# Edge stage of a graph network: three engines go by pairs of tiles instead of single tiles

## Chip, cores and metric

The kernel runs on one core of one Trainium2 chip. The metric is device time in microseconds (us) of one execution; the chip's runs are given as a median with their lowest and highest value. The output must be that of the reference.

## What is computed

The kernel runs two layers of a graph transformer on 3,125 nodes with 256 features and 100,000 edges. The change touches one stage, the messages of the first layer along the edges. The part of the reference that it computes:

```
src, dst = (edge_index[0], edge_index[1])
ei = jnp.concatenate([x[src], edge_attr], axis=-1)
core = jnp.maximum(ei @ W1 + b1, 0.0) @ W2 + b2
gate = jax.nn.sigmoid(ei @ Wg + bg)
msg = gate * core
agg = jax.ops.segment_sum(msg, dst, num_segments=x.shape[0])
```

Everything else (node tables before it, attention, experts, the second layer) is left as it is.

## The kernel before, in words

`stage_edges` works on 784 tiles of 128 edges (`NET`), four of them in a super (`SUP`), 16 in the body of a loop (`BODY`). The part of the products that depends on the source node lies ready in a table in memory; a tile's rows are gathered from it. Per tile t the work is:

- GpSimd: gather of 128 table rows of 512 numbers (`pool_pass`, L357), into eight slots.
- TensorE `edge_part` (L368, L369): the edge attributes times the weights, two matmuls of 512 columns into one of two PSUM banks.
- VectorE `whole_row` (L469): adds the gathered row, gives Z. With the first tile of a super it also copies the indices of the super after next (`indices`, L461).
- TensorE `turn` (L376): two transposes of the hidden half of Z into one of two PSUM banks.
- ScalarE `high` (L436): relu of it, rounded. ScalarE `gates` (L443): sigmoid of the other half of Z. ScalarE `seed` (L421): writes the bias into the PSUM bank that `core` adds to.
- VectorE `hidden_lo` (L482): what the rounding left over.
- TensorE `core` (L387): six matmuls of 256 columns.
- VectorE `message` (L507): gate times core.
- TensorE `total` (L404): adds the messages to the window of destination nodes, by a one-hot matrix; these two fp32 matmuls show as four records of 64 columns in the trace.

Once per super VectorE builds the one-hot matrices (`near_hots_of`, L499), adds the finished window to the sums (`add_window`, L519), and finishes the attributes of the super after next (`attr_lo`, L475), after ScalarE has rounded them (`rounded`, L451). TensorE's `edge_part` of that super's first tile waits for this L475.

The order is written out by hand: each engine runs `step(k, u)` for every u, and a step does its parts for tiles at fixed distances ahead of u or behind it. Nothing but these steps and the semaphores sets the order. Before the change a step is one tile. TensorE does `turn` of tile u+2, `total` of u-2, `core` of u, `edge_part` of u+4. VectorE does `message` of u-1, `whole_row` of u+3, `hidden_lo` of u+1, then what is due once per super. ScalarE does `high` of u+2, `seed` of u+1, `gates` of u+2. The semaphores let `turn` of tile t begin when `whole_row` of t and `hidden_lo` of t-2 are done, since two tiles share a bank.

Of the kernel before, what the change touches and what calls it, by code (L numbers as in the profile page):

```python
# [262 lines left out]
def stage_edges(c, tag, e):  # L263
# [11 lines left out]
    with ctx:  # L275
# [38 lines left out]
        def loop(step):  # L314


            def whole(eng):
                for u in range(-4, BODY):
                    step(0, u)
                with eng.Fori(1, NB - 1) as k:  # L320
                    for u in range(BODY):
                        step(k, u)
                for u in range(BODY + 3):
                    step(NB - 1, u)
            return whole

        def at(k, u):

            k, u = k + u // BODY, u % BODY
            if isinstance(k, int) and not 0 <= k < NB:  # L330
                return None
            return k, u, k * BODY + u, k * (BODY // SUP) + u // SUP, u // SUP, u % SUP

        def turn_of(k, j):

# [25 lines left out]
        def pe_pass(pe, s, p):  # L361
# [45 lines left out]
                last.then_inc(s["hot_used"], 1)  # L407

            def step(k, u):
                for ahead, part in ((2, turn), (-2, total), (0, core), (4, edge_part)):  # L410
                    a = at(k, u + ahead)
                    if a:
                        part(a)
            loop(step)(pe)

        def act_pass(act, s, p):
            def seed(a):

                k, u, i, sp_, j, q = a
                act.wait_ge(s["msg_ready"], p * NET + i + SLOTS - 1)  # L420
                act.activation(c.ps[4 + u % 2][:, 0:D], b2[:, :], ACT.Copy).then_inc(s["seeded"], 1)  # L421

            def step(k, u):
                a, next_core = at(k, u + 2), at(k, u + 1)
                if a:
                    high(a)
                if next_core:
                    seed(next_core)
                if a:
                    gates(a)  # L430

            def high(a):
                k, u, i, sp_, j, q = a
                act.wait_ge(s["z_turned"], p * NET + i + SLOTS + 1)
                act.wait_ge(s["core_ready"], p * NET + i + 1)
                act.activation(hT_hi[:, u % SLOTS, :, :].rearrange("p b n -> p (b n)"),  # L436
                               c.ps[2 + u % 2][:, 0:KB * 128], ACT.Relu).then_inc(s["h_rounded"], 1)
# [18 lines left out]
        def dve_pass(dve, s, p):  # L456
# [38 lines left out]
            def near_hots_of(a):  # L495

                k, u, i, sp_, j, q = a
                c.fence(dve)
                dve.tensor_tensor(near_hot[:, j % 2, :, :], bc(wide_iota[:, 0:WIN], 1, SUP),  # L499
                                  bc(rel[:, bass.ds(sp_ * SUP, SUP)], 2, WIN), ALU.is_equal).then_inc(s["hot_ready"], 1)  # L500
# [18 lines left out]
                dve.tensor_tensor(cols, cols, acc, ALU.add).then_inc(s["added"], 1)  # L519

            def step(k, u):
                for ahead, part in ((-1, message), (3, whole_row), (1, hidden_lo)):
                    a = at(k, u + ahead)
                    if a:
                        part(a)
                if s is sems[0]:
                    a = at(k, u)
                    if a and a[5] == 0:
                        near_hots_of(a)
                else:  # L530
                    a = at(k, u - 1)
                    if a:
                        far_hot_of(a)

                a = at(k, u)
                if a and a[5] == 2 and not (isinstance(a[0], int) and a[3] + 2 >= NSUP):
                    attr_lo(a[3] + 2, a[4])
                a = at(k, u - 3)
                if a and a[5] == SUP - 1:
                    add_window(a)  # L540
# [2671 lines left out]
```

## Time and profile before

| | us |
|---|---|
| median of 3 runs | 4462.46 |
| lowest and highest | 4461.76 and 4466.28 |
| the profiled execution, its own time | 4470.01 |
| its span, first to last instruction | 4468.2 |
| tiles of this stage, first and last transpose (L376) | 152.3 to 1637.9 |

Busy shares over the whole span: TensorE matmuls 84%, VectorE 66%, ScalarE 47%, GpSimd 48%. The mean granted TensorE clock is 0.905. The stage of the change fills the third of the span from 150 to 1640 us. Rows below name engines as PE (TensorE matmul), PEld (TensorE weight load), DVE (VectorE), ACT (ScalarE), POOL (GpSimd) and SPq (DMA issued by SyncE). In a timeline a row gives start, duration, engine, line, what is written and read, and in brackets idle time of the engine before it with what ended it. The ends of matmuls are modelled, so distances between their starts are what counts.

### The profile page before, as it was taken

What the parts mean: (1) busy time and instruction counts of PE and PEld (TensorE: products, weight loads), DVE (VectorE), ACT (ScalarE), POOL (GpSimd) and SP (SyncE); (2) the same over time, 40 slices, a digit from 0 to 9 for tenths busy, and PEclk for the clock granted to TensorE, in tenths of its full rate; (3) what the DMA queues carried; (4) which work ended last, traced back from release to release, by engine and by line L of the source; (5) the groups of instructions that cost most, each with busy time, mean ns of one, the idle gap of its engine ahead of it and who ended that gap; (6) DMA issues with size and microseconds to landing.
All of it is one profiled execution on the core that took longest, in us unless ns stands there. A gap on an engine that the chain in (4) does not pass through costs nothing. (4 is left out here: it accounts for less than half of the span.)

```text
span 4468.2 us, 86099 instructions
## 1 busy us (share of the span) xinstructions
PE 3749.2 (84%) x22567; PEld 3100.1 (69%) x22567; DVE 2969.3 (66%) x6849; ACT 2099.8 (47%) x4956; POOL 2147.9 (48%) x2102
## 2 busy tenths in 40 slices
PE   7899999999999987998996755556554669999996
PEld 6798988989898986997883433333332558888885
DVE  7699988989998987555332323223231469989998
ACT  3466655656665645774221100000000258888884
POOL 0355555555555521000005666666666257777872
PEclk9899999999999997999998977777876679999998
DMA  4465665666665630003553333333333123332325
GB/s 137 134 176 171 173 174 169 176 171 176 172 177 169 174 97 17 19 14 118 183 184 113 90 90 90 90 90 89 92 88 92 46 68 72 72 74 67 72 51 129
DMA packets 226995, 509.02 MB, mean 114 GB/s; under 512 B 51805, under 2 KB 94299, under 8 KB 220426
## 3 DMA queue, kind: packets, MB, share of 16 engines
q0 software_dynamic: 116736, 313.66, 25.2%
q1 hardware_dynamic: 106389, 187.30, 14.8%
q10 hardware_dynamic: 3679, 5.79, 0.4%
q8 instruction: 87, 1.43, 0.1%
q14 instruction: 104, 0.85, 0.1%
HBM read 434.08 MB, written 72.49 MB: 113 GB/s over the span
## 5 line engine op out<-in xcount | busy, mean ns | idle before, releaser
L775 POOL DMA_INDIRECT big<-table,e_idx x784 | 752.5, 960 | 978.7 <-DVE e_idx L866 589.1
L357 POOL DMA_INDIRECT big<-table,e_idx x784 | 768.4, 980 | 852.2 <-DVE big L469 300.8
L2315 POOL DMA_INDIRECT g_S<-gsrc,g_idx x512 | 608.9, 1189 | 216.5 <-issue 166.4
L436 ACT ACTIVATE e_hT_hi<-psum 128x256 fp32r<-128x256 f32 x784 | 301.1, 384 | 588.1 <-PE psum L376 496.3
L469 DVE TENSOR_TENSOR big<-psum,big 128x512 f32<-128x512 f32 x784 | 539.5, 688 | 45.6 <-PE psum L369 17.1
L896 DVE TENSOR_TENSOR big<-big,psum 128x128 f32 x196 | 56.6, 289 | 763.9 <-PE psum L802 324.5
L825 ACT ACTIVATE e_sums_kept<-psum 64x256 f32<-64x256 f32 x196 | 70.5, 375 | 1040.6 <-DMA gint<-big 429.6
L789 PE MATMUL psum<-big,e_near_hot 128*64 128x256 f32 x1568 | 500.2, 468 | 15.1 <-DMA big<-table,e_idx 14.8
L387 PE MATMUL psum<-e_w_hi,e_hT_hi 128*128 128x256 f32 x1568 | 509.7, 325 | 0.1
L387 PE MATMUL psum<-e_w_hi,e_hT_lo 128*128 128x256 f32 x1568 | 443.5, 283 | 0.0
L802 PE MATMUL psum<-ident,e_sums_kept 64*128 64x64 f32 x392 | 74.1, 278 | 439.4 <-ACT e_sums_kept L825 313.1
L387 PE MATMUL psum<-e_w_lo,e_hT_hi 128*128 128x256 f32 x1568 | 440.6, 281 | 0.0
L404 PE MATMUL psum<-e_near_hot,e_msg 128*128 128x64 f32 x3136 | 438.8, 263 | 0.2 <-DVE e_msg L507 0.2
L802 PEld LDWEIGHTS psum<-ident,e_sums_kept 64*128 64x128 f32 x392 | 45.6, 162 | 537.1 <-issue 537.1
L404 PEld LDWEIGHTS psum<-e_near_hot,e_msg 128*128 128x128 f32 x3136 | 414.3, 192 | 0.3 <-DVE e_msg L507 0.3
L507 DVE TENSOR_TENSOR e_msg<-psum,e_gate 128x256 f32<-128x256 f32 x784 | 331.0, 422 | 88.1 <-PE psum L387 42.8
L2860 PE MATMUL psum<-g_hot,g_spread 128*120 128x262 f32 x2048 | 345.3, 306 | 48.3 <-DVE g_spread L2694 22.7
L789 PEld LDWEIGHTS psum<-big,e_near_hot 128*64 128x64 f32 x1568 | 235.7, 165 | 179.0 <-issue 104.6
L2860 PEld LDWEIGHTS psum<-g_hot,g_spread 128*120 128x120 f32 x2048 | 282.0, 187 | 73.8 <-issue 55.2
L482 DVE SCALAR_TENSOR_TENSOR e_hT_lo<-psum,e_hT_hi 128x256 fp32r<-128x256 f32 x784 | 326.0, 416 | 0.1
L376 PE MATMUL psum<-ident,big 128*128 128x128 f32 x1568 | 305.1, 276 | 22.6 <-DVE e_hT_lo L482 20.7
L443 ACT ACTIVATE e_gate<-big 128x256 f32<-128x256 f32 x784 | 319.3, 407 | 0.0
(421 smaller groups left out, 9434.0 us busy)
## 6 DMA issues: line engine op xcount, KB each, us to landing
big<-in_attr_t SPq DMA_DIRECT2D x392, 128.0 KB
g_rest<-gpart SPq DMA_DIRECT2D x128, 256.0 KB
big<-table,e_idx POOLq DMA_INDIRECT x1568
table<-C SPq DMA_DIRECT2D x26, 896.0 KB
table<-n_rows SPq DMA_DIRECT2D x24, 896.0 KB
experts<-g_region SPq DMA_DIRECT2D x15, 560.0 KB
g_S<-gsrc,g_idx POOLq DMA_INDIRECT x512
table<-big SPq DMA_DIRECT2D x25, 224.0 KB
```

Source lines behind the costliest of these rows:

```text
L357: pool.indirect_dma_start(G[:, j % 2, q, :], None, table, bass.IndirectOffsetOnAxis(idx[:, j, q:q + 1], 0)).then_inc(s[f"G_in{j % 2}{q}"], 16)
L376: last = pe.transpose(c.ps[2 + u % 2][:, b * 128:(b + 1) * 128], Z[:, u % SLOTS, b * 128:(b + 1) * 128], c.ident[:, :])
L387: last = pe.matmul(c.ps[4 + u % 2][:, 0:D], x, y[:, b, :], start=False, stop=b == KB - 1 and x is lo, skip_group_check=True)
L404: last = pe.matmul(acc[:, b, :], msg[:, u % 2, b * 128:(b + 1) * 128], hot, start=q == 0 and (b == 0 or s is sems[1]), stop=q == SUP - 1, ...
L443: act.activation(gate[:, u % SLOTS, :], Z[:, u % SLOTS, D:2 * D], ACT.Sigmoid).then_inc(s["gate_ready"], 1)
L469: dve.tensor_tensor(Z[:, u % SLOTS, :], c.ps[u % 2], G[:, j % 2, q, :], ALU.add).then_inc(s["zs_ready"], 1)
L482: dve.scalar_tensor_tensor(out=hT_lo[:, u % SLOTS, :, :].rearrange("p b n -> p (b n)"), in0=c.ps[2 + u % 2][:, 0:KB * 128], scalar=0.0, in ...
L507: dve.tensor_tensor(msg[:, u % 2, :], c.ps[4 + u % 2][:, 0:D], gate[:, u % SLOTS, :], ALU.mult).then_inc(s["msg_ready"], 1)
L775: pool.indirect_dma_start(G[:, j % n, q, :], None, c.table1, bass.IndirectOffsetOnAxis(idx[:, j, q:q + 1], 0)).then_inc(s[f"G_in{j % n}"], 16)
L789: last = pe.matmul(near_sums(j), onehot[:, q, :], G[:, j % n, q, :], start=q == 0, stop=q == SUP - 1)
L2315: pool.indirect_dma_start(S[:, j, q, :], None, c.gsrc, bass.IndirectOffsetOnAxis(idx[:, j, 0, q:q + 1], 0)).then_inc(w_in[j], 16)
L2860: last = pe.matmul(sums[half], spread[:, j, 2 * u + p, half * CLASSES // 2:(half + 1) * CLASSES // 2, :].rearrange("p k c -> p (k c)"), ho ...
```

## The change

A helper `pair` runs a part for two tiles in a row, and the steps go over every second u. TensorE's step now does `edge_part` of u+4 and u+5, `turn` of u+2 and u+3, `total` of u-2 and u-1, `core` of u and u+1. ScalarE does `seed` of u and u+1, then `high` and `gates` of u+2 and u+3. VectorE does `message` of u-2 and u-1, `whole_row` of u+4 and u+5, `hidden_lo` of u+2 and u+3, then what is due once per super. Buffers, semaphores and their values, GpSimd's and SyncE's programs and the number of compute instructions stay.

```
             def whole(eng):
-                for u in range(-4, BODY):
+                for u in range(-6, BODY, 2):
                     step(0, u)
                 with eng.Fori(1, NB - 1) as k:
-                    for u in range(BODY):
+                    for u in range(0, BODY, 2):
                         step(k, u)
-                for u in range(BODY + 3):
+                for u in range(0, BODY + 4, 2):
                     step(NB - 1, u)
...
+        def pair(k, u, ahead, part):
+
+            for n in range(2):
+                a = at(k, u + ahead + n)
+                if a:
+                    part(a)
...
             def step(k, u):
-                for ahead, part in ((2, turn), (-2, total), (0, core), (4, edge_part)):
-                    a = at(k, u + ahead)
-                    if a:
-                        part(a)
+                for ahead, part in ((4, edge_part), (2, turn), (-2, total), (0, core)):
+                    pair(k, u, ahead, part)
             loop(step)(pe)
...
             def step(k, u):
-                a, next_core = at(k, u + 2), at(k, u + 1)
-                if a:
-                    high(a)
-                if next_core:
-                    seed(next_core)
-                if a:
-                    gates(a)
+                for ahead, part in ((0, seed), (2, high), (2, gates)):
+                    pair(k, u, ahead, part)
...
             def step(k, u):
-                for ahead, part in ((-1, message), (3, whole_row), (1, hidden_lo)):
-                    a = at(k, u + ahead)
-                    if a:
-                        part(a)
-                if s is sems[0]:
-                    a = at(k, u)
-                    if a and a[5] == 0:
-                        near_hots_of(a)
-                else:
-                    a = at(k, u - 1)
-                    if a:
-                        far_hot_of(a)
+                pair(k, u, -2, message)
+                if s is sems[1]:
+                    pair(k, u, -2, far_hot_of)
+                pair(k, u, 4, whole_row)
+                pair(k, u, 2, hidden_lo)
+                a = at(k, u)
+                if s is sems[0] and a and a[5] == 0:
+                    near_hots_of(a)
 
                 a = at(k, u)
                 if a and a[5] == 2 and not (isinstance(a[0], int) and a[3] + 2 >= NSUP):
                     attr_lo(a[3] + 2, a[4])
```

The order on TensorE, at the head of the loop's body (the step of u = 0). Before, the first tile's `turn` (L376) stands first:

```order
L376 MATMUL psum<-ident,big 128x128 x2
L397 ISA
L404 MATMUL psum<-e_near_hot,e_msg 128x64 x2
L383 REGISTER_ALU
L387 MATMUL psum<-e_w_hi,e_hT_hi 128x256
L387 MATMUL psum<-e_w_lo,e_hT_hi 128x256
L387 MATMUL psum<-e_w_hi,e_hT_lo 128x256
```

Three more L387 follow, and then `edge_part` (L368, L369) ends the step.

With the change, from the second `edge_part` of the step on (the first stands just ahead of these rows). In the changed kernel these lines have other numbers: L375 and L376 are `edge_part`, L383 is `turn`, L411 is `total`, L394 is `core`:

```order
L373 REGISTER_ALU
L375 MATMUL psum<-e_wb_hi,e_attr_parts 128x512
L376 MATMUL psum<-e_wb_lo,e_attr_parts 128x512
L381 REGISTER_ALU
L383 MATMUL psum<-ident,big 128x128 x2
L381 REGISTER_ALU
L383 MATMUL psum<-ident,big 128x128 x2
L404 ISA
L411 MATMUL psum<-e_near_hot,e_msg 128x64 x2
L404 REGISTER_ALU
L411 MATMUL psum<-e_near_hot,e_msg 128x64 x2
```

`edge_part` moved from the end of the step to its head, and every part stands there twice before the next part begins.

The order on VectorE in the step that finishes attributes (L475 in both kernels), before and then with the change; L507 is `message`, L469 `whole_row`, L482 `hidden_lo` in both:

```order
L507 TENSOR_TENSOR e_msg<-psum,e_gate 128x256
L465 REGISTER_ALU
L469 TENSOR_TENSOR big<-psum,big 128x512
L482 SCALAR_TENSOR_TENSOR e_hT_lo<-psum,e_hT_hi 128x256
L475 TENSOR_TENSOR e_attr_parts<-big,e_attr_parts 64x512
```

```order
L507 TENSOR_TENSOR e_msg<-psum,e_gate 128x256
L506 REGISTER_ALU
L507 TENSOR_TENSOR e_msg<-psum,e_gate 128x256
L465 REGISTER_ALU
L467 REGISTER_ALU
L469 TENSOR_TENSOR big<-psum,big 128x512
L465 REGISTER_ALU
L467 REGISTER_ALU
L469 TENSOR_TENSOR big<-psum,big 128x512
L482 SCALAR_TENSOR_TENSOR e_hT_lo<-psum,e_hT_hi 128x256 x2
L475 TENSOR_TENSOR e_attr_parts<-big,e_attr_parts 64x512
```

L475 now stands behind two `message`, two `whole_row` and two `hidden_lo` of its step instead of one each. Before, the `edge_part` that waits for it is the last part of the second tile step after it; now it is the first part of the next pair step.

## Rows read from the trace of the kernel before

**Rows 1.** Engines over the span (first part of the page), and the span:

```profile
span 4468.2 us, 86099 instructions
PE 3749.2 (84%) x22567; PEld 3100.1 (69%) x22567; DVE 2969.3 (66%) x6849; ACT 2099.8 (47%) x4956; POOL 2147.9 (48%) x2102
```

**Rows 2.** Windows: stretch, length, busy us of each engine (count), clock, DMA share, GB/s:

```profile
500.00:700.00 200.00, 197.61 (x1476) 179.93 (x1476) 180.88 (x423) 120.56 (x344) 103.03 (x106) 0.99 0.61 173
```

**Rows 3.** Waits, 200 to 1630 us: engine line <- releaser: us, times, longest:

```profile
DVE e_msg L507 <- PE psum L387: 38.5, 57, 3.2
PEld psum L376 <- DVE e_hT_lo L482: 38.4, 120, 2.8
...
PE psum L376 <- DVE e_hT_lo L482: 15.9, 9, 2.4
```

**Rows 4.** Timeline of TensorE, a little over one tile in which nothing stalls:

```profile
801.84 0.40 PE L368 MATMUL psum<-e_wb_hi,e_attr_parts 128*128 128x512 f32 x1
802.07 0.39 PE L369 MATMUL psum<-e_wb_lo,e_attr_parts 128*128 128x512 f32 x1
802.30 0.38 PE L376 MATMUL psum<-ident,big 128*128 128x128 f32 x2
802.52 0.56 PE L404 MATMUL psum<-e_near_hot,e_msg 128*128 128x64 f32 x4
802.89 0.36 PE L387 MATMUL psum<-e_w_hi,e_hT_hi 128*128 128x256 f32 x1
...
803.56 0.28 PE L387 MATMUL psum<-e_w_hi,e_hT_lo 128*128 128x256 f32 x1
803.57 0.19 PEld L368 LDWEIGHTS psum<-e_wb_hi,e_attr_parts 128*128 128x128 f32 x1
803.68 0.39 PE L368 MATMUL psum<-e_wb_hi,e_attr_parts 128*128 128x512 f32 x1
```

**Rows 5.** Timeline of TensorE, first tile of a loop body and of the next:

```profile
584.33 0.39 PE L368 MATMUL psum<-e_wb_hi,e_attr_parts 128*128 128x512 f32 x1
584.56 0.40 PE L369 MATMUL psum<-e_wb_lo,e_attr_parts 128*128 128x512 f32 x1
584.83 0.44 PE L376 MATMUL psum<-ident,big 128*128 128x128 f32 x2
585.11 0.56 PE L404 MATMUL psum<-e_near_hot,e_msg 128*128 128x64 f32 x4
...
586.27 0.39 PE L368 MATMUL psum<-e_wb_hi,e_attr_parts 128*128 128x512 f32 x1
...
614.04 0.39 PE L368 MATMUL psum<-e_wb_hi,e_attr_parts 128*128 128x512 f32 x1
```

**Rows 6.** Timeline of TensorE where another body begins, at half clock:

```profile
765.83 0.63 PE L369 MATMUL psum<-e_wb_lo,e_attr_parts 128*128 128x512 f32 x1
765.89 0.18 PEld L376 LDWEIGHTS psum<-ident,big 128*128 128x128 f32 x1 [0.15 <-DVE e_hT_lo L482]
```

**Rows 7.** Timeline of the three engines at a pause, one of seven:

```profile
560.02 0.40 PE L369 MATMUL psum<-e_wb_lo,e_attr_parts 128*128 128x512 f32 x1
561.34 0.42 DVE L507 TENSOR_TENSOR e_msg<-psum,e_gate 128x256 f32<-128x256 f32 x1 [3.10 <-PE psum L387]
561.36 0.38 ACT L436 ACTIVATE e_hT_hi<-psum 128x256 fp32r<-128x256 f32 x1 [3.30 <-remote]
562.81 0.44 PE L376 MATMUL psum<-ident,big 128*128 128x128 f32 x2 [2.39 <-DVE e_hT_lo L482]
```

**Rows 8.** Windows, one of five stretches at half clock behind a pause:

```profile
563.20:566.50 3.30, 3.30 (x16) 3.00 (x15) 1.89 (x6) 1.51 (x4) 1.89 (x2) 0.50 0.32 79
```

**Rows 9.** Timeline, VectorE, ScalarE and the transpose's weight load:

```profile
800.21 0.40 PE L369 MATMUL psum<-e_wb_lo,e_attr_parts 128*128 128x512 f32 x1
...
800.65 0.69 DVE L469 TENSOR_TENSOR big<-psum,big 128x512 f32<-128x512 f32 x1
...
801.26 0.41 DVE L482 SCALAR_TENSOR_TENSOR e_hT_lo<-psum,e_hT_hi 128x256 fp32r<-128x256 f32 x1
...
801.71 0.69 DVE L475 TENSOR_TENSOR e_attr_parts<-big,e_attr_parts 64x512 fp32r<-64x512 f32 x1
...
802.42 0.29 DVE L519 TENSOR_TENSOR big<-big,psum 128x128 f32 x1
...
802.63 0.42 DVE L507 TENSOR_TENSOR e_msg<-psum,e_gate 128x256 f32<-128x256 f32 x1
802.72 0.38 ACT L436 ACTIVATE e_hT_hi<-psum 128x256 fp32r<-128x256 f32 x1 [0.85 <-PE psum L376]
802.96 0.68 DVE L469 TENSOR_TENSOR big<-psum,big 128x512 f32<-128x512 f32 x1
803.56 0.41 DVE L482 SCALAR_TENSOR_TENSOR e_hT_lo<-psum,e_hT_hi 128x256 fp32r<-128x256 f32 x1
803.94 0.42 DVE L507 TENSOR_TENSOR e_msg<-psum,e_gate 128x256 f32<-128x256 f32 x1
804.03 0.27 PEld L376 LDWEIGHTS psum<-ident,big 128*128 128x128 f32 x2 [0.15 <-DVE e_hT_lo L482]
```

**Rows 10.** Groups of instructions, 200 to 1630 us: count, busy us, mean ns, idle before:

```profile
L499 DVE TENSOR_TENSOR e_near_hot<-big,e_rel 128x256 f32<-128x256 f32 x189 | 78.6, 416 | 0.0
L461 DVE COPY e_idx<-e_src_i 128x4 int32 x187 | 30.1, 161 | 0.0
```

## The prediction, made before the changed kernel ran

> **What bounds the kernel now.** I read the page first: over the span TensorE is busy 84% and VectorE 66% [rows 1], a mean over stages. The stage of the change is read by windows: in 200 us of its middle TensorE is busy 197.6 and VectorE 180.9 [rows 2], at a clock of 0.99. TensorE sets the pace there, with VectorE close behind. The 784 tiles take (1637.9 - 152.3) / 783 = 1.897 us each (first and last transpose, by the table above).
>
> The timeline says what of this is matmuls. A tile in which nothing stalls takes 803.68 - 801.84 = 1.84 us from L368 to L368 [rows 4]: 0.23 and 0.23 for `edge_part`, 0.22 for `turn`, 0.37 for `total` up to the first matmul of `core`, 0.79 for `core`. The loop body of 16 tiles shows one stall that always comes back: its first tile takes 586.27 - 584.33 = 1.94, the 15 after it 27.77, or 1.851 each [rows 5]. So 0.09 to 0.10 us per body is lost at L376, the transposes. The waits name what ends that: `hidden_lo` (L482) of two tiles earlier on VectorE, 120 waits of TensorE's weight load, 38.4 us by this view, which also counts what lies beside running matmuls [rows 3]. The matmul queue itself shows 15.9 us in 9 waits.
>
> Nearly all of those 15.9 us are something else: seven times in the stage, some 200 us apart, VectorE and ScalarE stand still for 3.1 to 3.3 us, and TensorE follows for about 2.4 [rows 7]. Behind five of them the clock falls to 0.50, its level of 1.2 GHz, for 3.3 us [rows 8]: 16 matmuls run where about twice as many would, some 1.7 us lost each.
>
> My account of the stage, over 783 x 1.84 = 1441 us: pauses 7 x 2.4 = 17, half clock 5 x 1.7 = 8.5, body stalls 49 x 0.1 = 4.9. The last 14 of 1485.6 are the filling of the pipe, and 0.01 us per tile of small waits and uneven starts.
>
> **The change, part by part.**
> - *Fewer changes between kinds of matmul.* Worth nothing. A step of two tiles has the same matmuls and weight loads, and none of the starts in [rows 4] has a gap that belongs to a change of kind: L369 to L376 takes 0.23, as L368 to L369 does, though the operand type changes there. The 0.37 of `total` is four records at some 0.11 with the first weight load of `core`, the next 0.79 is six matmuls at 0.12 and the rest of that load. A pair step is then 2 x 1.85 = 3.70 us, and twice the sum of its parts.
> - *`turn` no longer waits for VectorE.* I lay the pair step out from rows, with TensorE's step at 0. L369 of the two `edge_part` start at 0.23 and 0.70, `turn` at 0.93 and 1.15, the last `core` matmuls at 2.86 and 3.58. VectorE: `message` starts 0.38 after such a last matmul (803.56 to 803.94) [rows 4, 9], so at -0.46 and 0.26. `whole_row` can start 0.44 after L369 (800.21 to 800.65) [rows 9]: 0.67, the second 0.61 later at 1.28, `hidden_lo` at 1.89 and, 0.33 later (a short operation's spacing, 802.63 to 802.96), at 2.22. The transposes waiting for that `hidden_lo` come in the next step, at 3.70 + 0.93 = 4.63, and the signal takes 0.47 from its start (803.56 to 804.03) [rows 9]. Slack: 4.63 - 1.89 - 0.47 = 2.27 us, where now there is none in the stalled tiles. The body stalls go: -4.9. Of the small waits I give a third of 0.01 x 783, so -2.6.
> - *`edge_part` at the head of the step.* It waits for `whole_row` of two tiles earlier, 1.28 + 0.75 against 3.70 and more: free. Once per super (196 times) it waits for `attr_lo`, L475, and there the cover becomes thin. L475 starts 0.45 after the second `hidden_lo` (801.26 to 801.71) [rows 9]: 2.67, it takes 0.69 and 0.06 for the signal: 3.42. TensorE wants to load these weights 0.11 ahead of its matmul [rows 4], at 3.59. Slack 0.17 us, with 0 the value that I take. This is the wait that is late next.
> - *ScalarE.* `high` starts 0.31 after the second transpose (802.41, half way through the pair that starts at 802.30, to 802.72) [rows 4, 9]: 1.35, done at 1.73 and with the signal at 1.79, 0.10 ahead of the first `hidden_lo`. `seed` of the second tile follows its `message`, 0.26 + 0.42 + 0.06 = 0.74, done at 1.13; `core` of that tile begins at 2.9. Nothing waits.
> - *VectorE's load.* Per four tiles: 4 x (0.33 + 0.61 + 0.33) = 5.08, attributes and window 0.12 + 0.71 + 0.21 = 1.04 [rows 9], one-hot matrices 0.42 and indices 0.16 at most [rows 10]; 6.70 of 7.40 us. It keeps up, in whatever order.
> - *The loop's branch* was followed by `turn`, behind a matmul of 0.23; now it stands behind one of 0.12. Upper bound: weights are loaded 0.27 after L369's start [rows 5], which with 0.11 for the load would leave 0.26 open, 48 x 0.26 = +12.5. Lower bound 0. In one body `hidden_lo` was early and the load came 0.06 after L369's start [rows 6], so the branch itself is no longer than that; this is the nearest row: 0.06 + 0.11 - 0.12 = 0.05, at most 2.4 us. I take +1.2.
> - *Gathers and attribute transfers* keep their slots and semaphores. No wait of `whole_row` for a gather is among those of [rows 3], and GpSimd is busy 103 of 200 us [rows 2]. Cost 0.
> - *Pauses* stop all other engines; 0, bounded by -7 and +3. *Filling and draining* with pairs: two more `edge_part` ahead of the first `core`, less behind the last; I take +0.1, bounds -2 and +2.
>
> Sum: -4.9 - 2.6 + 1.2 + 0.1 = **-6.2 us**. Against the profiled execution's 4470.0 that is 4463.8; this execution is 7.5 above the median, so the time I predict is 4462.5 - 6.2 = **4456.3 us**.
>
> A rule that speaks against it: VectorE's starts lie closer than its durations (0.61 for 0.69, 0.33 for 0.42) [rows 9]. The Trainium skill ("VectorE: DVE Perf Modes", section "The DRAIN you can't avoid") says that the next operation does not start until the pipe is empty. By that rule four tiles would take VectorE 7.68 us (full durations, worked out under rival 1) in either order, the change would gain nothing, and the time would stay 4462.5. The trace before, with four tiles in 7.40, does not agree; the rule has its chance within rival 1.
>
> **The rivals.**
> 1. *VectorE sets the pace once like operations stand in a row* (two `whole_row`, two `hidden_lo`). No row shows two of a kind in a row. If they need their full durations, four tiles take 4 x (0.42 + 0.69 + 0.42) + 0.69 + 0.29 + 0.42 + 0.16 = 7.68 us instead of 7.40. For it: the durations. Against: the mixed starts. In full that is 196 x 0.28 = +55, but at that length the kernel before would already go slower than it does. The spacing between like operations can be longer than mixed ones by a little, and 0.03 in a pair step, 392 x 0.015 of it on TensorE, eats the gain above. I give "gains and small costs cancel", 4459 to 4466, 0.18. The full price is left out as remote.
> 2. *L475 comes late at the head of the step*: slower. Place: TensorE's first load of every second pair step. It decides from the point where L475 starts later than 2.84 after the step's start, 0.17 later than laid out; a chain of three waits each 0.06 late does it. Price: 0.05 to 0.2 us x 196 = 10 to 39, less the 6 gained: 4466 to 4495, likeliest 0.1 late, 4476. For it: the thinnest cover of all, and VectorE often 0.08 behind its shortest spacing. Against: VectorE catches up 0.3 us in the pair step between. Chance 0.14.
> 3. *The pauses get shorter and the clock stays up.* With 1 to 2 us of slack in every buffer TensorE runs on while the others stand: 7 x 1 us, and without a gap as long five stretches of half clock may go, 8.5. Then 4456 - 7 - 8.5 = 4441. For it: slack grows from 0 to 2.27 at the transposes. Against: the slack at L475 does not grow, and VectorE must still make good 3 us of work. Chance 0.15.
> 4. *The change does not do what it says*: the order of instructions shows that it does. Under 0.01.
>
> **How the numbers follow.** Forecast 0.53, its own range 4451 to 4461; rival 1 0.18, rival 2 0.14, rival 3 0.15. A measurement of this kernel can tell 0.2% from no change, 8.9 us. Faster by more than that is under 4453.5: rival 3 and a third of the forecast's share, 0.15 + 0.18 = 0.33. Slower by more is over 4471.4: most of rival 2 and a remnant of full price of rival 1, 0.15. Within: 0.52. The range reaches half into rivals 2 and 3: 4443 to 4475.
>
> **What would show it.** Right: 16 tiles in 29.5 to 29.6 us in stretches without a pause (29.71 now), no wait of `turn` for `hidden_lo` except at pauses, seven pauses of TensorE of 2 to 2.6 us. Wrong: a group of waits of `edge_part` for L475, some 98 or 196 of them (rival 2); VectorE without idle time and `total` or `core` waiting for it (rival 1); a first `edge_part` of each body 0.2 us late (the branch); the clock at 1.00 throughout (rival 3). The forecast would fall if two like operations on VectorE start more than 0.65 and 0.37 apart.

## The result, and the profile after

| | before | after |
|---|---|---|
| median, us | 4464.37 (4 runs) | 4595.03 (4 runs) |
| lowest and highest, us | 4461.76 and 4469.42 | 4578.25 and 4603.06 |
| profiled execution's span, us | 4468.2 | 4576.5 |
| first and last transpose of the stage, us | 152.3 and 1637.9 | 153.0 and 1756.6 |

The changed kernel takes 1.028 times as long, 95% interval 1.0261 to 1.0299: slower by 131 us by the medians, where 6 us less were forecast. The profiled execution, the shortest of its four, is 108.3 longer in its span. This stage alone is 1603.7 us long instead of 1485.6, by 118.0: a tile takes 2.048 us instead of 1.897.

Engines over the span, from the page of the changed kernel (as [rows 1]):

```profile
span 4576.5 us, 86146 instructions
PE 3769.2 (82%) x22567; PEld 3125.5 (68%) x22567; DVE 2927.9 (64%) x6849; ACT 2081.3 (45%) x4956; POOL 2135.6 (47%) x2102
```

The same stretch as in [rows 2], stretch, length, busy us of each engine, clock, DMA share, GB/s:

```profile
500.00:700.00 200.00, 188.87 (x1388) 172.94 (x1387) 164.86 (x397) 112.23 (x325) 93.25 (x99) 1.00 0.57 161
```

TensorE runs 1388 matmuls where it ran 1476, and stands for 11 of 200 us; the others do some 6% fewer instructions too. No engine is the bound any more, and the clock is not the cause: it is 1.00. The waits, 200 to 1630 us (as [rows 3]: us, times, longest), with `turn` now L383, `edge_part` L375, `core` L394, `total` L411:

```profile
ACT psum L426 <- DVE e_msg L507: 429.9, 194, 3.5
...
DVE e_msg L507 <- PE psum L394: 88.7, 87, 1.7
PEld psum L411 <- DVE e_msg L507: 83.6, 109, 1.0
...
PE psum L411 <- DVE e_msg L507: 57.9, 103, 0.8
DVE e_msg L507 <- issue: 57.5, 59, 1.7
...
PEld psum L375 <- issue: 33.7, 55, 1.1
...
PE psum L375 <- DVE e_attr_parts L475: 20.6, 27, 0.9
...
PE psum L383 <- DVE e_hT_lo L482: 2.0, 2, 1.7
```

The waits of `turn` for `hidden_lo` are gone, as forecast: 2 are left. What replaces them is a ring: TensorE's `total` waits for `message`, and `message` (L507) waits for `core`, or for "issue", where the profile shows no releaser at all. The timeline shows what that is, here in one super:

```profile
861.39 0.94 POOL L364 DMA_INDIRECT big<-table,e_idx  x1 [2.74 <-DVE big L469]
...
862.64 0.94 POOL L364 DMA_INDIRECT big<-table,e_idx  x1 [0.30 <-issue]
...
863.03 1.00 PE L411 MATMUL psum<-e_near_hot,e_msg 128*128 128x64 f32 x8
...
864.13 0.94 POOL L364 DMA_INDIRECT big<-table,e_idx  x1 [0.56 <-issue]
...
864.52 0.29 PE L394 MATMUL psum<-e_w_hi,e_hT_lo 128*128 128x256 f32 x1
...
865.36 0.29 DVE L519 TENSOR_TENSOR big<-big,psum 128x128 f32 x1
865.38 0.95 POOL L364 DMA_INDIRECT big<-table,e_idx  x1 [0.30 <-issue]
...
867.28 0.76 DVE L507 TENSOR_TENSOR e_msg<-psum,e_gate 128x256 f32<-128x256 f32 x2 [1.63 <-issue]
...
867.76 1.10 PE L411 MATMUL psum<-e_near_hot,e_msg 128*128 128x64 f32 x8 [0.66 <-DVE e_msg L507]
```

The last matmul of the first tile's `core` starts at 864.52. By [rows 4, 9] `message` follows 0.38 later; here 2.76 later, after VectorE stood still for 1.63 us. The trace also records each semaphore's updates. Around that time they read (modelled end of the instruction that signals, update, difference, us):

```
total, second tile     864.03   867.102   3.07
core, first tile       864.805  867.194   2.39
core, second tile      865.524  867.270   1.75
edge_part, first       866.200  867.313   1.11
edge_part, second      866.665  867.355   0.69
turn, first            866.883  867.398   0.52
VectorE L475           865.330  865.340   0.01
VectorE L519           865.649  865.659   0.01
```

**TensorE's completion signals are held and then come in a burst**, while it computes on and VectorE's signals are on time. The usual difference is 13 ns. I count as one hold all neighbouring signals of TensorE, in the order of their instructions, that are over 0.25 us late, and name it by its longest lag. From 200 us to the end of the stage there are 152 holds over 1 us after, and 7 before: the seven pauses of [rows 7]. They go with the gathers: GpSimd starts four gathers within 4.5 us 164 times after (861.39 to 865.38 above) and 7 times before, each time ahead of a pause, and about nine in ten of these fours after have a hold over 1 us within 8 us. Shorter holds are there before too: 160 of 0.25 to 0.85 us, nearly all behind two gathers that start 1.25 to 1.5 us apart. One of the seven pauses, in the timeline of the kernel before:

```profile
351.39 0.95 POOL L357 DMA_INDIRECT big<-table,e_idx  x1 [1.27 <-DVE e_idx L461]
355.46 0.96 POOL L357 DMA_INDIRECT big<-table,e_idx  x1 [3.12 <-issue]
356.72 0.95 POOL L357 DMA_INDIRECT big<-table,e_idx  x1 [0.30 <-issue]
357.97 0.95 POOL L357 DMA_INDIRECT big<-table,e_idx  x1 [0.30 <-DVE e_idx L461]
359.22 0.94 POOL L357 DMA_INDIRECT big<-table,e_idx  x1 [0.30 <-issue]
...
361.21 0.42 DVE L507 TENSOR_TENSOR e_msg<-psum,e_gate 128x256 f32<-128x256 f32 x1 [3.17 <-PE psum L387]
```

GpSimd stands for 3.12 us, makes up for it with four gathers in a row, and the pause follows.

### The profile page after: what moved, and what is told of

Same layout as the page of the kernel before. It is cut to its first block and busy times, and to the rows that moved or that the text cites. A ratio compares the mean times of both kernels' runs of the same rounds, so it can differ in the third digit from the quotient of the medians.

```text
span 4576.5 us, 86146 instructions
## 1 busy us (share of the span) xinstructions
PE 3769.2 (82%) x22567; PEld 3125.5 (68%) x22567; DVE 2927.9 (64%) x6849; ACT 2081.3 (45%) x4956; POOL 2135.6 (47%) x2102
## 5 line engine op out<-in xcount | busy, mean ns | idle before, releaser
L364 POOL DMA_INDIRECT big<-table,e_idx x784 | 745.8, 951 | 992.2 <-DVE big L469 695.7
L771 POOL DMA_INDIRECT big<-table,e_idx x784 | 751.5, 959 | 978.5 <-DVE e_idx L862 587.6
L426 ACT ACTIVATE psum<-e_b 128x256 f32<-128x256 f32 x784 | 286.6, 388 | 621.9 <-DVE e_msg L507 482.5
L469 DVE TENSOR_TENSOR big<-psum,big 128x512 f32<-128x512 f32 x784 | 517.1, 683 | 38.1 <-PE psum L383 12.4
L394 PE MATMUL psum<-e_w_hi,e_hT_hi 128*128 128x256 f32 x1568 | 475.4, 303 | 0.5 <-issue 0.5
L411 PE MATMUL psum<-e_near_hot,e_msg 128*128 128x64 f32 x3136 | 408.9, 273 | 65.6 <-DVE e_msg L507 62.7
L411 PEld LDWEIGHTS psum<-e_near_hot,e_msg 128*128 128x128 f32 x3136 | 383.1, 192 | 94.9 <-DVE e_msg L507 91.0
L394 PE MATMUL psum<-e_w_hi,e_hT_lo 128*128 128x256 f32 x1568 | 441.8, 282 | 0.0
L394 PE MATMUL psum<-e_w_lo,e_hT_hi 128*128 128x256 f32 x1568 | 441.3, 281 | 0.0
L507 DVE TENSOR_TENSOR e_msg<-psum,e_gate 128x256 f32<-128x256 f32 x784 | 301.4, 418 | 215.8 <-PE psum L394 98.3
L375 PE MATMUL psum<-e_wb_hi,e_attr_parts 128*128 128x512 f32 x784 | 324.6, 414 | 29.3 <-DVE e_attr_parts L475 24.0
L482 DVE SCALAR_TENSOR_TENSOR e_hT_lo<-psum,e_hT_hi 128x256 fp32r<-128x256 f32 x784 | 297.4, 414 | 40.8 <-ACT e_hT_hi L436 29.3
L436 ACT ACTIVATE e_hT_hi<-psum 128x256 fp32r<-128x256 f32 x784 | 261.7, 377 | 110.8 <-PE psum L383 69.8
```

The costliest lines, as they stand in the source:

```text
L364: pool.indirect_dma_start(G[:, j % 2, q, :], None, table, bass.IndirectOffsetOnAxis(idx[:, j, q:q + 1], 0)).then_inc(s[f"G_in{j % 2}{q}"], 16)
L375: pe.matmul(c.ps[u % 2], tile, wb_hi[:, :], start=True, stop=False)
L394: last = pe.matmul(c.ps[4 + u % 2][:, 0:D], x, y[:, b, :], start=False, stop=b == KB - 1 and x is lo, skip_group_check=True)
L411: last = pe.matmul(acc[:, b, :], msg[:, u % 2, b * 128:(b + 1) * 128], hot, start=q == 0 and (b == 0 or s is sems[1]), stop=q == SUP - 1, ...
L469: dve.tensor_tensor(Z[:, u % SLOTS, :], c.ps[u % 2], G[:, j % 2, q, :], ALU.add).then_inc(s["zs_ready"], 1)
L482: dve.scalar_tensor_tensor(out=hT_lo[:, u % SLOTS, :, :].rearrange("p b n -> p (b n)"), in0=c.ps[2 + u % 2][:, 0:KB * 128], scalar=0.0, in ...
```

## The experiments

Sets of runs met chips in different condition, so each is compared with the kernel before in its own set. That took 4261.4 us in the first, 4473.5 in the second, 4549.7 in the third, 4551.7 in the fourth and 4471.6 in the fifth, on the same chip as the third. The theories, put up after the result: A, signals are held when gathers start close together; B, TensorE's own new order holds them; C, the condition of the chip does; from the fourth set on also D, indirect transfers hold them at any spacing. "Fours" are starts of four gathers within 4.5 us, from 200 us on; holds are those over 1 us, from 200 us on. Several runs compute something else than the kernel, and serve for their time alone: e4 and e10 gather only half of each row and from another table, e11 and e15 load the same 512 rows over and over in place of those that the indices name, e12 uses the attributes of the first 16 tiles throughout.

| run | us | ratio, 95% interval | us per tile | fours | holds |
|---|---|---|---|---|---|
| e1 | 4266.14 | 1.0013 (1.0004 to 1.0022) | 1.849 | 25 | 0 |
| e2 | 4264.03 | 1.0005 (0.9995 to 1.0015) | 1.856 | 191 | 0 |
| e3 | 4261.90 | 1.0002 (0.9992 to 1.0012) | 1.856 | 13 | 0 |
| e4 | 4259.88 | 0.9991 (0.9981 to 1.0001) | 1.849 | 14 | 0 |
| e5 | 4593.46 | 1.0269 (1.0240 to 1.0299) | 2.061 | 170 | 170 |
| e6 | 4525.33 | 1.0108 (1.0083 to 1.0133) | 1.966 | 7 | 84 |
| e7 | 4745.72 | 1.0609 (1.0587 to 1.0631) | 2.254 | 184 | 189 |
| e8 | 4729.27 | 1.0568 (1.0546 to 1.0590) | 2.233 | 2 | 5 |
| e9 | 4683.94 | 1.0288 (1.0260 to 1.0316) | 2.079 | 108 | 146 |
| e10 | 4675.76 | 1.0272 (1.0239 to 1.0304) | 2.078 | 163 | 166 |
| e11 | 4496.64 | 0.9867 (0.9832 to 0.9902) | 1.849 | none made | 0 |
| e12 | 4671.67 | 1.0257 (1.0220 to 1.0294) | 2.076 | 169 | 175 |
| e13 | 4873.84 | 1.0716 (1.0696 to 1.0736) | 2.337 | 0 | 0 |
| e14 | 4900.83 | 1.0766 (1.0743 to 1.0789) | 2.356 | 0 | 0 |
| e15 | 4503.00 | 0.9904 (0.9880 to 0.9928) | 1.856 | none made | 0 |
| e16 | 4692.44 | 1.0311 (1.0287 to 1.0335) | 2.102 | 171 | 176 |
| e17 | 4441.74 | 0.9931 (0.9918 to 0.9945) | 1.856 | 0 | 4 |
| e18 | 4448.71 | 0.9941 (0.9928 to 0.9955) | 1.864 | 0 | 6 |

**First set: nothing to see.** e1 is the changed kernel with the gather of each odd tile waiting for a message as well:

```
                         pool.wait_ge(s["zs_ready"], p * NET + sup * SUP + q + 1)
+                        if q % 2 and not (isinstance(k, int) and j * SUP + q < 9):
+                            pool.wait_ge(s["msg_ready"], p * NET + sup * SUP + q - 8)
```

> The changed kernel with one wait more on GpSimd: the gather of every odd tile also waits for the message (L507) of the tile 13 before it, which comes about 2.3 us after the whole_row that frees its slot, so that the two gathers of a pair no longer go back to back. Theory A (four gathers issued within 4.5 us make TensorE's completion signals come up to 3 us late, once per super, and VectorE and ScalarE wait for them): the late signals go, a pair step takes 3.70 us throughout, time 4450 to 4462 us. Theory B (the order by pairs on TensorE itself holds the signals back, the gathers are only late because of it): no change, 4575 to 4605 us.

e2 is the kernel before with the four gathers of a super back to back, e3 with gathers in pairs (`q - q % 2 + 2`):

```
-                        pool.wait_ge(s["zs_ready"], p * NET + sup * SUP + q + 1)
+                        pool.wait_ge(s["zs_ready"], p * NET + sup * SUP + SUP)
```

> The kernel before, order by single tiles kept; only GpSimd waits with all four gathers of a super until the last whole_row that frees their slots, so that they go back to back, 1.25 us apart. Theory A: late signals in nearly every super, up to 196 of them, each 1.5 to 2.5 us on TensorE: 4700 to 4950 us. Theory B: the order on TensorE is that of before, gathers have over 5 us of slack: 4460 to 4475 us.

> The kernel before, with GpSimd's gathers in pairs back to back, pairs 3.7 us apart (four within 6.2 us). Theory A with its bound at 4.5 us: no late signals beyond the seven of before, 4460 to 4470 us. If two gathers back to back are already enough: 4550 and more. Theory B: 4460 to 4470 us.

e4 gathers half as many bytes in the changed kernel:

```
-                        pool.indirect_dma_start(G[:, j % 2, q, :], None, table,
+                        pool.indirect_dma_start(G[:, j % 2, q, 0:D], None, c.i["x"],
```

> The changed kernel, but the gather takes rows of 256 numbers from the input x instead of 512 from the table: it leaves out the node part of the gate and takes other numbers for the hidden part, as many descriptors, half the bytes. Theory A in the form 'too many gathered bytes in a short time': late signals gone or rare, 4450 to 4480 us. Theory A in the form 'too many descriptors or issues by GpSimd': as the changed kernel, 4575 to 4605 us. Theory B: the same, 4575 to 4605 us.

No run had a late signal, though e2 made 191 fours and A had expected 4700 us or more for it: as A was first put, for any chip, it fell here. The condition of the chip has a part in it, and these four runs can't tell A from B. They show one thing more: in e4, with the order of the change and nothing held, half of the gathers start less than 1.35 us behind the one before, but only 14 fours come of it.

**Second set.** e5 is the changed kernel unedited, e6 and e7 are e1 and e2 again. In e8 VectorE's order is message, row, message, hidden low part, row, hidden low part:

```
-                pair(k, u, -2, message)
-                pair(k, u, 4, whole_row)
-                pair(k, u, 2, hidden_lo)
+                for ahead, *row in ((-2, message, *far), (4, whole_row), (-1, message, *far), (2, hidden_lo),
+                                    (5, whole_row), (3, hidden_lo)):
```

> The changed kernel itself, nothing edited, beside the kernel before on whatever chip this is. On the chip of the four runs before this one (before 4261 us, no pauses of the machine in its edge stage) no variant lost anything. Theory A (signals of TensorE come late whenever four gathers start within 4.5 us): ratio 1.028 again on any chip, some 130 to 145 holds of up to 3.1 us between the end of a `total` matmul and VectorE's next `message`, 2.04 us for a tile. Theory B (TensorE's own new order makes them late): the same here, and the next run but one decides. Theory C (the late signals belong to a chip, or to the state of it, that also shows the seven pauses in the kernel before): 1.028 if the kernel before takes 4464 us here, and 0.998 to 1.003 with 1.85 us for a tile if it takes 4261 us.

> The changed kernel in which the gather of an odd tile also waits for the message of the tile 13 before it, so that the four gathers of a super are spaced by more than 4.5 us; TensorE, ScalarE and VectorE are as changed. Theory A: the holds are gone, ratio 0.995 to 1.003, 1.85 us for a tile, also where the unedited change loses. Theory B: holds stay, ratio about 1.028 where the unedited change has 1.028. Theory C: like the unedited change on this chip, which alone says nothing between A and B if that has no holds.

> The kernel before with the four gathers of each super issued back to back (each waits for the Z row of the super's last tile); TensorE, ScalarE and VectorE as before. Theory A: holds once for each super on a chip where the change loses, ratio 1.02 to 1.04. Theory B: no holds, ratio 0.999 to 1.003. Theory C with a chip that has no pauses: 1.000 to 1.002 again.

> The changed kernel with VectorE's order message, row, message, hidden low part, row, hidden low part: the two rows of a pair, and with them the release of G and the starts of gathers and edge parts, lie over 1 us further apart; TensorE and ScalarE keep the order of the change. Theory A: fewer windows with four gathers in 4.5 us and with them fewer holds, ratio 0.998 to 1.015 where the change has 1.028. Theory B: holds stay, 1.02 to 1.04. In either case without holds 1.85 to 1.88 us for a tile, ratio 0.998 to 1.005.

The loss repeats. e7 decides between A and B: TensorE's order is that of before, only the gathers are bunched, and it loses 6.1% (A had expected 2 to 4%) with 189 holds, one for nearly each four. So the new order of TensorE isn't needed for the loss, and B falls. The same program in two conditions, windows of e2 and then of e7:

```profile
600.00:1000.00 400.00, 400.00 (x3017) 365.23 (x3016) 371.67 (x863) 247.66 (x700) 208.97 (x215) 1.00 0.61 177
```

```profile
600.00:1000.00 400.00, 344.89 (x2486) 298.38 (x2485) 306.30 (x712) 204.73 (x578) 168.01 (x177) 1.00 0.50 145
```

TensorE never stops in e2 and is busy 345 of 400 us in e7. So C holds as well, as a condition: bunched gathers cost only where the chip holds signals.

e6 missed what A expected, no holds and no loss. It has next to no fours and 60% less loss, but still 84 holds over 1 us (3.5 at the longest) and 348 over 0.25 us, where e5 has 170 and 195. Its gathers still start in pairs 1.25 us apart. Four close gathers are thus not needed for a late signal; two will do, with a shorter one. e8 missed too: it has 5 holds and loses more than the change, because its order made a new ring, in which ScalarE's `seed` and the attributes come late at each super. Its waits, 200 to 1700 us:

```profile
ACT psum L426 <- DVE e_msg L507: 667.8, 598, 2.4
...
DVE e_hT_lo L482 <- ACT e_hT_hi L436: 180.4, 239, 0.8
...
PE psum L375 <- DVE e_attr_parts L475: 131.0, 165, 1.1
```

It has 2 fours and few holds, as A has it, but says nothing on what holds cost. It does show what rival 2 of the prediction feared, in another kernel than the changed one: TensorE at the head of the step waits for L475, 165 times.

**Third set: what in the gathers does it.** e9 spaces odd gathers by `h_ready` in place of `msg_ready`. e10 is e4 again. In e11 SyncE loads consecutive rows in plain transfers, and GpSimd makes none:

```
+                    for q in range(SUP):
+                        sp.wait_ge(s["zs_ready"], p * NET + sup * SUP + q + 1)
+                        sp.dma_start(G[:, j % 2, q, :], table[q * 128:(q + 1) * 128, :]).then_inc(
+                            s[f"G_in{j % 2}{q}"], 16)
```

In e12 the attributes are loaded for the first 16 tiles only, and then SyncE just signals:

```
-                        sp.dma_start(attr[half * DE:(half + 1) * DE, j % 2, :],
+                    sp.sem_inc(s[f"attr_in{j % 2}"], 32)
```

> The changed kernel in which the gather of every odd tile also waits for the hidden low part of the tile ten before it, so that gathers start about 1.5 and 2.2 us apart instead of in pairs; TensorE, ScalarE and VectorE keep the order of the change. What counts depends on the chip: on one where the kernel before takes over 4450 us the signals of TensorE come late, on one where it takes 4261 us none did. Theory A (late signals follow from gathers that start close together): on a chip of the first kind nearly all holds over 1 us gone and a ratio of 0.997 to 1.004 (the spacing by messages, which still let pairs start 1.1 us apart, gave 1.0108, the unedited change 1.0269). Theory B (the new order of TensorE or VectorE makes them late whatever the gathers do): 1.008 to 1.03. On a chip of the second kind both 0.998 to 1.003.

> The changed kernel with gathers of 256 columns of x instead of 512 of the table (the other half of G is cleared once, so Z lacks the gathered second half and the table's first): as many indirect transfers at the same moments with as many rows, half the bytes. On a chip with late signals: if the bytes of close gathers count, the holds shrink by more than half, ratio below 1.012; if the number of rows or the making of the indirect transfers counts, they stay, 1.02 to 1.03. On a chip without late signals 0.998 to 1.002, as it had there before (0.9991).

> The changed kernel in which SyncE loads 128 consecutive rows of the table by a plain transfer in place of each indirect one of GpSimd (the rows are the wrong ones; as many bytes, released by the same Z rows). On a chip with late signals: if it is GpSimd's making of indirect transfers that delays TensorE's signals, no holds and a ratio of 0.995 to 1.002; if it is the traffic into SBUF, holds as in the change, 1.02 to 1.03. On the other kind of chip 0.997 to 1.003.

> The changed kernel without the transfers of attributes after the first 16 tiles (SyncE only signals, the attributes of the first tiles are used throughout): the gathers are as in the change. On a chip with late signals: if close gathers alone cause the holds, 130 or more of them stay and the ratio is 1.02 to 1.03; if it is the sum of both kinds of traffic, the ratio falls below 1.012. On the other kind of chip 0.997 to 1.002.

Half the bytes (e10) and no attribute traffic (e12) change nothing: 1.0272 and 1.0257. Without GpSimd's indirect transfers (e11) every late signal is gone, and the kernel beats the one before by 1.3%. e11 changes several things at once, the engine and the queue that the transfers come from, how they are made and which rows they read, and no run tells which of these counts. Its window, to be read against those above:

```profile
600.00:1000.00 400.00, 400.00 (x3023) 375.48 (x3023) 366.05 (x865) 246.16 (x702) 0.00 (x0) 1.00 0.57 177
```

e9 missed what A expected. Its gathers were not spaced: 108 fours. It waits for another engine's progress, and after a hold that engine catches up and releases gathers in a bunch, which goes before the next hold. This and e6 speak for spacing by time.

**Fourth set.** e13 (changed) and e14 (before) clear a scratch tile after each gather and wait for that; e15 is the kernel before with e11's plain transfers; e16 is the changed kernel unedited.

```
+                        pool.memset(pace[:, :], 0.0).then_inc(s["paced"], 1)
+                        pool.wait_ge(s["paced"], p * NET + sup * SUP + q + 1)
```

> The changed kernel in which GpSimd clears a scratch tile of 128 x 384 after every gather and waits for that, which sets starts of gathers at least 1.6 us apart by time and not by the progress of another engine (a clear of 128 x 2048 took 1.81 us, so this one about 0.4). On a chip where the unedited change loses 2.7%: theory A (TensorE's signals come late when four gathers start within some 4.5 us): no holds over 1 us, ratio 0.996 to 1.003. A rival, D (GpSimd's making of indirect transfers delays the signals also when they are evenly spaced, and pairs of tiles only make the delays matter): holds stay, 1.010 to 1.028. On a chip without late signals both 0.998 to 1.003.

> The kernel before with the same clear and wait after every gather. Its seven pauses follow four gathers made back to back after GpSimd stood still. Theory A: they are gone or much shorter, ratio 0.993 to 0.999 on a chip that has them. Theory D, or pauses that come first and make the gathers bunch: they stay, 0.999 to 1.003. On a chip without late signals 0.999 to 1.003.

> The kernel before with the gathers replaced by plain transfers of 128 consecutive rows of the table, issued by SyncE (wrong rows, as many bytes), as in the earlier run of the changed kernel, which gave 0.9867 with no late signal. It has the order of before, so the two together give what the change is worth when no signal is late. If the prediction's sum for the pairs was right (6 us gained), this is at 0.1 to 0.2% above the changed one, 0.988 on a chip like that one; if the pairs gain nothing by themselves, the same 0.987; if indirect transfers had cost nothing in the kernel before, 0.998 to 1.002.

> The changed kernel, unedited, on this chip, as a measure for the paced one. Ratio 1.024 to 1.030 where the chip has late signals, 0.997 to 1.003 where it has none (the kernel before at about 4261 us).

The pacing was mis-sized. GpSimd in e13:

```profile
1002.35 0.95 POOL L365 DMA_INDIRECT big<-table,e_idx  x1 [0.86 <-POOL e_pace L368]
1003.30 0.43 POOL L368 MEMSET e_pace<- 128x384 f32 x1
1004.59 0.95 POOL L365 DMA_INDIRECT big<-table,e_idx  x1 [0.86 <-DVE big L472]
```

Once it has waited, a gather begins 0.86 us after the clear, so a gather takes 2.24 us at least, more than the 1.85 of a tile, and GpSimd bounds both kernels: both expectations of the times missed. But not one signal of TensorE was over 0.25 us late in either, in a set in which the unedited change (e16) has 176 holds: gathers that slow hold nothing. With plain transfers the changed kernel takes 1.849 us per tile (e11) and the one before 1.856 (e15).

**Fifth set.** e17 and e18 use two scratch tiles in turn and wait two gathers later, ahead of the gather, so that GpSimd doesn't stand:

```
+                        pool.wait_ge(s["paced"], p * NET + sup * SUP + q + 1)
                         pool.sem_inc(begun_gathering, 1)
...
+                        pool.memset(pace[:, q % 2, :], 0.0).then_inc(s["paced"], 1)
```

> As the paced changed kernel, but the clear of 128 x 384 (0.43 us) after each gather goes to two scratch tiles in turn and is waited for only two gathers later, so GpSimd doesn't stand 0.86 us before each gather as it did there (2.25 us for a gather at least, which bound that kernel). Starts of gathers should be at least 0.95 + 0.43 + 0.30 = 1.68 us apart, four of them at least 5.0 us, and GpSimd can keep up with 1.85 us for a tile. Theory A (late signals need gathers closer than this): on a chip where the kernel before takes over 4450 us hardly a hold over 1 us, ratio 0.990 to 1.004, where the unedited change had 1.027 to 1.031. Theory D (indirect transfers delay the signals at any spacing below 2.2 us, and pairs make it matter): 1.010 to 1.03. On a chip with 4261 us both 0.998 to 1.003.

> The kernel before with the same clear after each gather, waited for two gathers later. Theory A: the seven pauses after four gathers in a row lose their late signals, ratio 0.991 to 0.999 on a chip that has them (the kernel before with plain transfers had 0.9904 on one). Theory D: 0.999 to 1.005. If this is as fast as the paced changed kernel within 0.3%, the pairs themselves are worth nothing here; if it is 0.1 to 0.3% slower, they are worth what was forecast.

Both beat the kernel before, by 0.69% and 0.59%. GpSimd in e17, and its window:

```profile
1004.50 0.95 POOL L366 DMA_INDIRECT big<-table,e_idx  x1 [0.50 <-DVE big L472]
1005.45 0.43 POOL L369 MEMSET e_pace<- 128x384 f32 x1
1006.05 0.95 POOL L366 DMA_INDIRECT big<-table,e_idx  x1 [0.16 <-issue]
```

```profile
500.00:700.00 200.00, 200.00 (x1513) 187.75 (x1512) 183.07 (x433) 123.17 (x351) 149.34 (x217) 1.00 0.61 177
```

Gathers start 1.55 us apart at least, four in 4.65. TensorE does not stop in the 200 us in which it stood for 11 after the change. A holds, D falls. One reserve: the unedited change was not run in this set. That signals are held on this chip is taken from the third set and from the time of the kernel before, 4471.6 us, near the 4464 and 4473 of the sets in which the change lost 2.7% and more. e17 beats both kernels and is the version to keep; over e18 it gains 7.0 us, which the two intervals alone don't separate, but the lengths of the stage do (below).

## Why the prediction was wrong, step by step

**The step that failed** is *Gathers and attribute transfers keep their slots and semaphores ... Cost 0.* I asked whether a row waits for its gather, and it does not. I didn't ask what the moments of the gathers do to others. `whole_row` of two tiles in a row releases two gathers 1.25 us apart: half of the starts are less than 1.35 us behind the one before (375 of 753), where the kernel before has 51. Behind such pairs TensorE's signals are held, VectorE stands, catches up, and two pairs close up to a four, which is held for longer. That the bunch costs time is shown, 6.1% in the kernel before (e7), and that spacing by time removes the loss (e17). That the fours come of the holds is read from e4 against e10, the same program: 372 and 378 close starts, but 14 fours where nothing is held and 163 where signals are.

The plain runs split the 118 us. Against 1447.7 us for the stage in e11, the changed stage is 156.0 longer. Against 1453.1 in e15, the stage before is 32.5 longer. So the gathers cost 123.5 us more with the change, and the pairs themselves gain 5.4 (e11 over e15). The two give 118 by the way they are worked out, which tests nothing. What it rests on is that the plain runs' stages would be as long on the first chip. The stages of e1 and e2 on another chip, without late signals, are: 1447.8 and 1453.2.

- *`turn` no longer waits*: right. In e17 16 tiles take 29.65 us at the median of their starts, before 29.74, so 0.09 for each of 49 bodies; 29.65 is just short of the 29.5 to 29.6 that I had named as the sign of being right. All gains of the pairs together, forecast as 6.2, are 5.4 (e11 over e15) and 1459.9 - 1453.2 = 6.7 (e18 over e17).
- *`edge_part` at the head, slack 0.17*: right where nothing else is late. e17 has one wait of TensorE for L475's successor, 0.6 us. The 27 waits after the change follow holds. Rival 2 gave the right sign for a wrong reason, and its price of 10 to 39 us was too low.
- *VectorE*: right. Two rows in a row take 1.29 us together, so the second starts 0.61 after the first; two hidden low parts take 0.75, so 0.33. Rival 1 falls. The rule that I quoted from the Trainium skill ("VectorE: DVE Perf Modes", section "The DRAIN you can't avoid") does not describe these starts either, but the section itself excepts instructions that are not held, which start earlier; I had left this out.
- *Pauses, 0, bounded by -7 and +3*: wrong as a separate thing. (The 17 us that I counted are also above the 15.9 of the waits: 2.4 is the longest stop, not the mean.) I took them for stops of the machine, all engines at once, and didn't look at GpSimd ahead of them. They are holds of TensorE's signals behind four gathers back to back. In e18, without fours, the stage takes 1459.9 us, 25.7 less than before (1485.6), and no clock falls; I had counted 17 for pauses and 8.5 for half clock. The holds under 1 us of the kernel before go as well, from 160 to 5. Rival 3 was worth more than I gave, by a change that I hadn't thought of. Its sign, a clock of 1.00, came with the change too (200 to 1600 us, before 0.99), and no gain with it.
- *The loop's branch*, +1.2, can't be told from 0: the bodies' 29.65 are 16 x 1.853, and the tile without a stall takes 1.84 to 1.85.

My range ended at 4475 because I bounded each cost of a new order by the engines' own rows, and took no row in which gathers start close together and asked what comes behind it. The seven pauses and the short holds in the trace before were such rows.

## What to carry to other kernels

When a change makes an engine do like things in a row, look also at what that releases: transfers bunch with it, and on all chips met here but one GpSimd's indirect ones then made another engine's signals late. Where a wait names no releaser, or a consumer starts long after the producer's last instruction, compare the semaphore's update with the producer's end. If transfers must be spaced, space them by time on the engine that issues them, since a wait for another engine's progress gives way just when that engine catches up (e6, e9).

## What the runs showed of the hardware that I had not expected

- TensorE's signals came up to 4.8 us after the modelled end of their instruction (e16; 4.7 in the changed kernel at 809 us), in order and in a burst, and ScalarE's and VectorE's in the same stretch after 10 ns. Where the stage begins, behind ten gathers and more in a row, it was 7.9 us with the change and 5.1 before. This needs GpSimd's indirect transfers: none with plain transfers (e11, e15), none at 2.24 us for a gather (e13, e14), 4 holds at 1.55 or more (e17), 84 of mostly 1 us with pairs 1.25 apart and hardly a four (e6), 176 where fours come within 4.5 us (e16).
- It depends on the condition of the chip: 191 fours without a late signal in e2, 184 fours with 189 holds in e7. Only one chip showed none, that of the first set, so the condition can be that chip's own. The unedited change was not run where none occurs; the nearest are e1 and e4, 1.0013 and 0.9991. What that condition is, and on which path the signals are held, stays open.
- A gather of 128 rows keeps GpSimd 0.95 us with 512 columns as with 256 (959 and 946 ns in e10's two gather loops). The Trainium skill ("DMA: Bandwidth & Descriptors", section "Anatomy of one DMA — SWDGE (gpsimd) path") calls the making of descriptors small and says that one can emit many before the cost of more shows; in these rows GpSimd's part is half of a tile's time, and closely spaced gathers made TensorE's signals late. Its section "Latency and other measured facts" offers as a best guess for why two of the DMA engines are usually slower that the descriptor rings of this path load ports of SBUF; no run here can show whether the held signals have to do with that.
- Waiting two gathers later for the clear turned 2.24 us for a gather into 1.55. A wait for GpSimd's own last instruction cost 0.86 us ahead of a gather, which otherwise starts 0.16 to 0.30 after the instruction before.
